# A positional conv split between VectorE, ScalarE and GpSimd, and a Winograd unit started before the last attention jobs are done

## What is computed

```
x = x + depthwise_conv3x3(x, pos_w) + pos_b            # positional conv
blk = mean over 8 x 8 blocks of x (49 per image)
scores = lin(gelu(lin(blk, s1)), s2); idx = top 4 of the 49
y_cmp = mha(x, blk, blk);  y_sel = mha(x, blk[idx], blk[idx])
y_win = attention of each pixel over its 7 x 7 window (edge padded)
g = softmax(lin(layernorm(x), g_w))                     # three gates
y = g0 * y_cmp + g1 * y_sel + g2 * y_win + x
t = depthwise_conv3x3(lin(y, pin_w), dw_w)              # 128 -> 512 channels
x1, x2 = halves of t
out = layernorm(y + lin(gelu(x1) * x2, pout_w))
```

## Time and profile before

| | |
|---|---|
| median of 3 runs | 791.99 us (790.29 to 796.1) |
| the profiled execution | 791.16 us |
| its span | 789.1 us |
| TensorE matmul busy | 691.7 us (88%) |
| VectorE busy | 571.2 us (72%) |
| ScalarE busy | 393.0 us (50%) |
| GpSimd busy | 213.0 us (27%) |

### The profile page before, as it was taken

The page is one execution under the profiler, slowest core; times in us unless marked ns, Lnnn a source line. Parts: engine busy times, 40 slices in busy tenths (PEclk is TensorE's granted clock), DMA queues, the critical chain, the costliest instruction groups (busy, mean ns, idle before and its releaser), DMA issues.

```text
span 789.1 us, 19122 instructions
## 1 busy us (share of the span) xinstructions
PE 691.7 (88%) x7549; PEld 461.3 (58%) x7549; DVE 571.2 (72%) x860; ACT 393.0 (50%) x855; POOL 213.0 (27%) x365
## 2 busy tenths in 40 slices
PE   3979899999888788898888788888799999999994
PEld 2557477777566666675666566666444555455552
DVE  6982788888898675565675565666158989999942
ACT  2077777676764244343444344445333152547565
POOL 2050255555653014411111101111710436200000
PEclk9989999999999897878989896989699999999998
DMA  5000245555489887767777677651100000001001
GB/s 233 0 1 1 67 124 151 148 142 143 139 156 173 185 153 138 136 125 131 141 146 151 129 133 143 136 99 46 37 2 0 0 1 0 1 20 42 20 20 61
DMA packets 81605, 72.50 MB, mean 92 GB/s; under 512 B 11586, under 2 KB 80107, under 8 KB 81006
## 3 DMA queue, kind: packets, MB, share of 16 engines
q1 hardware_dynamic: 61358, 47.03, 24.9%
q10 hardware_dynamic: 20160, 24.26, 16.7%
HBM read 47.39 MB, written 21.57 MB: 87 GB/s over the span
## 4 chain that ended last, share of the span: by engine, by line
PE 45%; DVE 22%; ACT 12%; DMA 8%; issue 8%; ACTq 3%; SPq 2%; DVEq 0%
PE banks L938 13%; PE banks L761 8%; PE banks L871 6%; DVE FP L1212 5%; DMA Q<-nT 5%; PE banks L856 4%; DVE mx L1356 3%; DVE wn L1321 3%; ACTq L355 3%; DVE AC L1212 2%; ACT SEB L1063 2%; PE banks L889 2%; PE banks L834 2%; DMA FP<-nT 2%; ACT banks L1043 1%
## 5 line engine op out<-in xcount | busy, mean ns | idle before, releaser
L1321 DVE TENSOR_REDUCE wn<-banks 112x2 f32<-112x560 f32 x224 | 164.3, 739 | 89.9 <-PE banks L761 87.4
L1088 ACT ACTIVATE P<-banks 98x448 f32<-98x448 f32 x224 | 119.2, 541 | 149.5 <-PE banks L856 118.1
L938 PE MATMUL banks<-FP,PTB 128*128 128x392 f32 x384 | 129.4, 493 | 1.0 <-DVE c L1344 0.9
L1212 DVE SCALAR_TENSOR_TENSOR AC<-XT,vec,AC 128x1540 f32<-128x1540 f32 (+5 forms) x48 | 115.1, 2400 | 1.1
L871 PE MATMUL banks<-P,Vw 84*17 84x56 f32 (+1 forms) x3584 | 97.5, 232 | 8.8 <-ACT OB L1101 6.9
L938 PEld LDWEIGHTS banks<-FP,PTB 128*128 128x128 f32 x384 | 72.8, 190 | 55.5 <-DVE c L1344 1.6
L761 PE MATMUL banks<-K,Q 126*112 126x280 bf16 x288 | 71.6, 335 | 9.0 <-DVE wn L1321 8.6
L856 PE MATMUL banks<-Q,K 128*128 128x56 bf16 x1152 | 60.8, 197 | 17.4 <-DMA Q<-nT 12.7
L856 PEld LDWEIGHTS banks<-Q,K 128*128 128x128 bf16 x1152 | 56.0, 104 | 28.0 <-DMA Q<-nT 15.5
L871 PEld LDWEIGHTS banks<-P,Vw 84*17 84x17 f32 (+1 forms) x3584 | 57.5, 104 | 20.6 <-issue 9.7
L504 POOL TENSOR_TENSOR pk<-pr,pk 128x434 bf16<-128x434 f32 (+1 forms) x42 | 42.8, 1018 | 89.9 <-ACT pk L1033 89.9
(11 more groups left out here) (228 smaller groups left out, 1140.8 us busy)
## 6 DMA issues: line engine op xcount, KB each, us to landing
K<-k_parts ACTq DMA_DIRECT2D x24, 434.0 KB, 5.4
k_parts<-pk SPq DMA_DIRECT2D x28, 325.5 KB, 4.6
Vw<-v_rows SPq DMA_DIRECT2D x112, 52.1 KB
Q<-q_parts ACTq DMA_DIRECT2D x48, 112.0 KB, 6.0
FP<-k_parts ACTq DMA_DIRECT2D x12, 434.0 KB, 5.3
Vw<-v_rows SPq DMA_DIRECT2D x112, 44.6 KB
q_parts<-pk SPq DMA_DIRECT2D x14, 336.0 KB, 2.6
v_rows<-vst SPq DMA_DIRECT2D x14, 263.5 KB
```

The costliest lines, as they stand in the source:

```text
L938: last = mm(bank(2 + place_in_unit, C, ZPIX), WT[:, dy, part, C * grp:C * (grp + 1)], D[:, part, QROWS * q + dy:QROWS * (q + 1) + dy, :].r ...
L1088: a(P[q % 4][0:HKEYS[half], :], PS[0:HKEYS[half], 4 + q % 2, 0:HEADS * SUB], ACT.Exp).then_inc(sem("w_exp"), 1)
L1212: return ve.scalar_tensor_tensor(out=o, in0=src(ro + dy, rn, co + dx, cn), scalar=v(wcol + t), in1=o, op0=ALU.mult, op1=ALU.add)
L1321: ve.tensor_reduce(wn[tl % 2][:, 2 * hp:2 * hp + 2], src, AX.X, ALU.max, negate=True).then_inc(sem("w_slot_read"), 1)
```

## The change

**Positional conv.** TensorE takes four bands of image 1 (`PEB` = 4) and VectorE the last three. Of image 0 VectorE does the first 32 rows (`SPLIT`). The last 24 rows, three bands, are started by ScalarE with the scaled copy, and for each of eight taps ScalarE writes a product into one of two buffers (`products`, in `PTB`), which GpSimd adds onto `FP`. GpSimd's three summing additions go; VectorE sums both images along the rows, after both convs. GpSimd copies image 1 into `XT`, and ScalarE only image 0.

**Feed-forward.** The first conv unit's four parts and the first part of unit 1 are issued inside the loop over the steps, around the last two jobs' D and Y. `outputs(0)` stands in VectorE's loop ahead of job 13's D. The last slots and the first `pin_bands` use other PSUM banks.

```diff
-        PEB = 5
+        PEB = 4
+        SPLIT = 4 * BLOCK
 ...
# GpSimd
+            outer = FP[:, 0, PAD + SPLIT:PAD + SIDE, PAD:PAD + SIDE]
+            for n, t in enumerate(SIDE_TAPS):
+                dy, dx = TAPS[t]
+                rn, co, cn = SIDE - SPLIT - max(0, dy), max(0, -dx), SIDE - abs(dx)
+                pool.wait_ge(sem("diag"), 9 + n + 2)
+                pool.wait_ge(sem("consts"), 5 + n)
+                o = outer[:, 0:rn, co:co + cn]
+                g.tensor_tensor(o, o, products[n % 2][:, 0:rn, co:co + cn], ALU.add).then_inc(sem("consts"), 1)
 ...
-                if m == 0:
-                    by2 = FP[:, 0, mid, mid].rearrange("p r (n e) -> p r n e", e=2)
 ...
+            for b in range(BANDS):
 ...
+                g.tensor_copy(dst, src).then_inc(sem("tile_order1"), 1)
 ...
# TensorE
+                if q == STEPS + 9:
+                    pe.wait_ge(sem("w_exp"), STEPS)
+                    pe.wait_ge(sem("w_slot_read"), pa_order["Y", JOBS - 3] + 1)
+                    pe.wait_ge(sem("wt_ready"), 2)
+                    pe.wait_ge(sem("d_border"), 1)
+                    pe.wait_ge(sem("d_ready"), 2)
+                    conv_part(0, 0)
+                    conv_part(0, 1)
                 if q == STEPS + 11:
+                    conv_part(0, 2)
                     pe.wait_ge(sem("w_y"), JOBS - 1)
-                    pe.wait_ge(sem("w_exp"), STEPS)
-                    pin_bands(0, 0, (4, 5))
+                    pe.wait_ge(sem("w_out"), SUBS * JOBS)
+                    pin_bands(0, 0, (6, 7), range(3))
+                    conv_part(0, 3)
+                    pin_bands(0, 0, (6, 7), range(3, BANDS))
+                if q == STEPS + 25:
+                    conv_part(1, 0)
 ...
-            pe.wait_ge(sem("w_y"), JOBS)
-            pe.wait_ge(sem("wt_ready"), 2)
-            pe.wait_ge(sem("d_border"), 1)
-            pe.wait_ge(sem("t_read"), BANDS)
 ...
# ScalarE
+            act.wait_ge(sem("x0_loaded"), 16)
+            x0 = X[:, 0, :].rearrange("p (r c) -> p r c", c=SIDE)
+            a(FP[:, 0, PAD + SPLIT:PAD + SIDE, PAD:PAD + SIDE], x0[:, SPLIT:, :], ACT.Identity, scale=c1[:, 0:1], bias=v(V_POSB)).then_inc(sem("diag"), 1)
+            for n, t in enumerate(SIDE_TAPS):
+                dy, dx = TAPS[t]
+                rn, co, cn = SIDE - SPLIT - max(0, dy), max(0, -dx), SIDE - abs(dx)
+                if n >= 2:
+                    act.wait_ge(sem("consts"), 5 + n - 1)
+                a(products[n % 2][:, 0:rn, co:co + cn], x0[:, SPLIT + dy:SPLIT + dy + rn, co + dx:co + dx + cn], ACT.Copy, scale=v(V_POSW + t)).then_inc(sem("diag"), 1)
 ...
+                if n in (2, 4):
+                    pos_read(n // 2 - 1)
+            pos_read(2)
 ...
# VectorE
-                first = BLOCK * PEB if m else 0
+                first, end = (BLOCK * PEB, SIDE) if m else (0, SPLIT)
 ...
+                    dve.wait_ge(sem("consts"), 5 + len(SIDE_TAPS))
                     dve.wait_ge(sem("pos_read"), PEB)
 ...
+            for m in range(IMAGES):
+                inner = FP[:, m, PAD:PAD + SIDE, PAD:PAD + SIDE]
+                ve.tensor_reduce(bs1[:, m, :, :], inner.rearrange("p r (b c) -> p r b c", c=BLOCK), AX.X, ALU.add).then_inc(sem("conv_done"), 1)
 ...
+                if q == STEPS + 12:
+                    outputs(0)
```

More of the change, by code:

```diff
@@ L195, in build @@
         TP = SEB[:, 0:9 * HID].rearrange("p (y x o) -> p y x o", y=3, x=3)
+        products = [PTB[:, n * 24 * SIDE:(n + 1) * 24 * SIDE].rearrange("p (r c) -> p r c", c=SIDE) for n in range(2)]
         def xt(img):
@@ L824, in _, with pin_bands @@
             pe.wait_ge(sem("w_zeroed"), 1)
-            def pin_bands(m, grp, banks):
+            def pin_bands(m, grp, banks, bands=range(BANDS)):
                 at0 = BANDS * (IMAGES * m + grp)
@@ L830, in pin_bands @@
                     pe.wait_ge(sem("t_read"), at0)
-                for b in range(BANDS):
+                for b in bands:
                     if b >= 2:
@@ L834, in pin_bands, with conv_part @@
                     mm(bank(banks[b % 2], C, BAND), w("pin", C, C * grp), X[:, m, b * BAND:(b + 1) * BAND], start=True, stop=True).then_inc(sem("t_proj"), 1)
[L836 removed]
+            def conv_part(u, place_in_unit):
+                n, grp = divmod(u, 2)
+                q, part = n % QUARTERS, WINO[place_in_unit]
+                if u >= 1:
+                    pe.wait_ge(sem(("x2_m1", "x2_sums", "x2_even", "x2_odd")[place_in_unit]), u)
+                for dy in range(3):
+                    last = mm(bank(2 + place_in_unit, C, ZPIX), WT[:, dy, part, C * grp:C * (grp + 1)],
+                              D[:, part, QROWS * q + dy:QROWS * (q + 1) + dy, :].rearrange("p r c -> p (r c)"), start=(dy == 0), stop=(dy == 2))
+                last.then_inc(sem("x2_m"), 1)
+            for q in STEP_RANGE:
+                if q == STEPS + 9:
[6 more added lines that the diff above has]
+                    conv_part(0, 1)
                 if q == STEPS + 11:
+                    conv_part(0, 2)
                     pe.wait_ge(sem("w_y"), JOBS - 1)
[L839 to L840 removed]
+                    pe.wait_ge(sem("w_out"), SUBS * JOBS)
[4 more added lines that the diff above has]
+                    conv_part(1, 0)
                 if q == 1:
@@ L924, in z_variance @@
                 last.then_inc(sem("z_var"), 1)
-            for u in range(UNITS):
-                n, grp = divmod(u, 2)
-                m, q = divmod(n, QUARTERS)
+            for u in range(1, UNITS):
+                m, q = divmod(u // 2, QUARTERS)
                 pe.wait_ge(sem("d_ready"), QUARTERS * m + min(q + 2, QUARTERS))
-                for place_in_unit, part in enumerate(WINO):
+                for place_in_unit in range(int(u == 1), len(WINO)):
                     if place_in_unit == 2 and u - 1 in ZAT:
@@ L934, in _ @@
                         z_centre(ZAT[u])
[L935 to L940, removed]
+                    conv_part(u, place_in_unit)
                 if u in PINS:
+                    pe.wait_ge(sem("w_y"), JOBS)
                     pin_bands(*PINS[u], (0, 1))
@@ L966, in _, with tile_order, pos_read @@
                 a(diag[:, t, :], cst[:, CI:CI + C], ACT.Copy, scale=c1[:, 0:1] if t == 4 else v(V_POSW + t)).then_inc(sem("diag"), 1)
[L968 to L971, removed]
+            def tile_order(first, last):
+                for b in range(first, last):
+                    src = FP[:, 0, PAD + BLOCK * b:PAD + BLOCK * (b + 1), PAD:PAD + SIDE].rearrange("p r (s c) -> p s r c", c=SUBC)
+                    dst = XT[:, 0, b * BAND:(b + 1) * BAND].rearrange("p (s r c) -> p s r c", s=SUBS, c=SUBC)
                     a(dst, src, ACT.Copy).then_inc(sem("tile_order"), 1)
-            act.wait_ge(sem("p_gl"), 1)
-            a(cgw[:, C:GW], PS[:, 7, 0:3], ACT.Copy).then_inc(sem("gl_copied"), 1)
-            for b in range(PEB):
+            def pos_read(b):
                 act.wait_ge(sem("pos_conv"), b + 1)
@@ L1485, in _ @@
                     product(ZAT[u])
-                outputs(u)
+                if u:
+                    outputs(u)
             next(todo, None)
```

79 lines of the change are left out of this document (37 added, 42 removed).

## The result

The median went from 791.87 to 805.23 us (four runs, 798.47 to 809.08), a ratio of 1.0154 with an interval of 1.0111 to 1.0196: 1.5% slower, and 4 us above the forecast of 801.0. It lies inside the range that was forecast (794 to 806), by 0.8 us. The profiled execution took 804.07 us, 12.9 more than that of before.

What follows compares the result with a forecast made beforehand. VectorE was taken to bound the positional conv; in the feed-forward part TensorE and VectorE both ran nearly without a gap. 791.16 + 8.0 (positional conv) + 1.8 (feed-forward) = 801.0 us, range 794 to 806.

Steps and rivals of the forecast that it cites:

- What bounds the first stage: Positional conv: VectorE is the bound until `blk_ready` at 56.9 us; TensorE's bands and GpSimd's sums end earlier.
- VectorE's own work, 31.8 us: Positional conv: VectorE's taps and scaled copies alone take 31.8 us after the change, where before it was 43.6.
- The additions cost their time: Positional conv: GpSimd's additions and VectorE's taps take turns, so all eight additions lengthen VectorE's chain, by 16.5 us.
- rival A: Positional conv: GpSimd's additions run beside the taps, so the conv gives -6.2 us and the total is near 785; chance 0.09.
- Their price, 16.5 us: Positional conv: eight additions of 10,442 elements at 1.76 ns each, less 1.8 us, cost VectorE 16.5 us.
- rival C: Positional conv: the new additions are slower than the old sums, +10.5 us and more, 803.5 to 807 in all; chance 0.15.
- The reductions, +3.3: Behind the convs: image 0's sums leave GpSimd and become a second long reduction on VectorE, adding 3.3 us.
- ScalarE's order and the copies into `XT`: First stage: waits between ScalarE and GpSimd hold nobody else, and GpSimd's padding and `XT` copies cost the reduction nothing.
- Edit 2, TensorE's lead: Feed-forward change: TensorE is 1.5 us ahead after three matmuls of unit 1, 3 if its clock comes back earlier.
- Edit 2, VectorE's taps +9.3: Feed-forward change: VectorE's taps begin 9.3 us later, `outputs(2)` ends +3.2, `outputs(5)` starts +1.9; the whole change costs +1.8.
- Rival B: Feed-forward: TensorE sets the pace and VectorE's late taps are absorbed, -1.5 to -3 us, 797 in all; chance 0.18.
- edit 1: The positional conv change as a whole: `blk_ready` and the kernel 8.0 us later, bounds -6.2 and +14.2.

Runs made afterwards that it cites:

- e9: e1 with VectorE's conv of image 0 held until GpSimd's eight additions are done; 821.44 us in one run.
- e3: e1 with each of GpSimd's eight additions replaced by a fill of the product buffer (output not the reference's); 785.18 us, ratio 0.9889 to the kernel before.
- e1: The kernel before with only the positional conv half of the change; 805.19 us, ratio 1.0143 to the kernel before.
- e2: The kernel before with only the feed-forward half of the change; 793.01 us, ratio 0.9996 to the kernel before.
- e4: The kernel before with GpSimd's three summing additions of image 0 moved behind the conv of image 1; 792.16 us, ratio 0.9974 to the kernel before.

## Why the prediction was right, step by step

*What bounds the first stage.* Right. TensorE and ScalarE had room, and VectorE's chain moved `blk` by what it was longer itself. That shift stays whole: the last `banks<-PTB,VP` matmuls before the window attention come 10.6 us later too.

*VectorE's own work, 31.8 us.* Right to 0.1: in e9 the two convs are 39.08 to 70.88.

*The additions cost their time (against rival A).* Right, and shown from both sides. With additions a tap is 2.4 us too long; with GpSimd only writing the product's buffers at the same places (e3) none is. The Trainium skill, SBUF — State Buffer, section "Who interferes with whom", has the port pair shared by VectorE and GpSimd as an exclusive lock. By that rule the additions are paid in full, and e1 and e9 agree, save for the 0.38 us. Beside two-input instructions it excepts GpSimd instructions that only write, and e3's taps agree with that too.

*Their price, 16.5 us.* This is the term that was mis-sized, and rival C, given 0.15, is what happened: 58.9 - 8.1 - 31.8 = 19.0 us, 2.4 each. I took 1.76 ns an element from the sums since they stood in the same stage and layout. Nothing in them said that another pair of operands has the same price, and the nearest row with an own addition and other operands pointed up. By e9, the bound from the earlier trace rows was too high (2.78 us alone, where 2.35 ns would be 3.1). Theirs is most of the difference of 4 us between forecast and result: the first stage is +10.6 instead of +8.0.

*The reductions, +3.3.* Right: from 58.92 to 67.60 is 8.7 us, and before 51.57 to 57.02, 5.4.

*ScalarE's order and the copies into `XT`.* Right, they hid: GpSimd's copies run beside the reductions and end at 63.9, and TensorE's wait is for `blk`.

*Edit 2, TensorE's lead.* Too small: 1.5 forecast, "3 if the clock comes back earlier", and it is 3.4 in e2. There the clock came back 6 us behind D (at 569), where I had counted 7.4, and the six matmuls took 6.7 us, where I had 7.5. In after the clock didn't fall at D at all, so the half clock "with conv matmuls in it" isn't there.

*Edit 2, VectorE's taps +9.3 and what follows.* Right in kind. From D of job 12 to the first tap it is 15.24 us in before, 22.8 in e2 (+7.6) and 20.7 in after. The wait ahead of `outputs(2)` is gone, as forecast, and TensorE is held from there. But `outputs(2)` ends only 1.4 us later in e2 instead of 3.2, and `outputs(5)` starts 0.4 later instead of 1.9, so edit 2 costs 0.0 to +0.5 instead of +1.8, by kernels with the same clock. The medians say +0.9 (ratio of after less that of e1) and -0.3 (e2), each give or take 3 to 5 us, and can't tell this from 1.8. Rival B, that the lateness is absorbed, is nearer here than my sum; but its gain of 1.5 to 3 us isn't there either, since the lead goes in three waits.

*The total.* By the stages it is 791.2 + 10.6 + 0.0 = 801.8, against 801.0 forecast. That they come so close is luck: edit 1 was taken 2.6 us too low and edit 2 some 1.5 too high. The profile has 804.1, since the window attention took 4.4 us more and the clock behind D gave back 1.9; the median has 805.2. The profile's 2.3 us over the stages lie where the forecast had no term, in the window attention, which spans 13.6 us over the twelve profiles; whether edit 1 has a share in it isn't settled, and the median's 3.4 us can't be placed.

## What to carry to other kernels

A two-input fp32 operation on GpSimd beside VectorE's two-input taps doesn't share their work here, it stands in their queue: giving GpSimd an element costs VectorE about 1.8 ns to save 1.05. Price such a hand-over by the other engine's duration with those operands alone, measured once, and not by another instruction's slope. Work moved into a waiting engine's gap pays only if the next reader keeps up: look for the engine that frees the buffers before counting the gap as gain. Compare a stretch only between profiles in which the clock was at the same level.

## What was not expected of the hardware

The 0.38 us: VectorE loses less than the whole addition, by the same amount at four sizes from 0.84 to 2.90 us (e4, e9). It fits that GpSimd's padding copies, which last 0.36 us alone, cost the taps nothing: beside four of them e9's eight taps took 12.88 us, 1.61 each. The copies did wait, a tap each. GpSimd in e9, one copy beside taps and one with none:

```profile
58.05 1.71 POOL L496 COPY FP<-FP 128x168 f32<-128x168 f32 x1
71.07 0.36 POOL L495 COPY FP<-FP 128x168 f32<-128x168 f32 x1 [8.04 <-DVE c L1244]
```

I had not thought of the scaled copy as something that GpSimd could hold, since it reads one tensor only. The one of 1,344 elements took 3.23 us in after beside an addition and 0.98 in e9 without one. The Trainium skill, SBUF — State Buffer, section "Who interferes with whom", counts a `tensor_scalar` in if it runs in a two-port mode; these two numbers agree. A fill held it too, unlike the taps: 1.29 us in e3. VectorE's timeline in e9:

```profile
56.93 0.98 DVE L1238 TENSOR_SCALAR FP<-X,c,vec 128x1344 f32<-128x1344 f32 x1
```

The contiguous addition is slower than the one with 55-element rows, 2.99 against 2.78 us for 1,320 elements.

TensorE's clock at the hand-over differs between profiles. With a pause of 3.55 us ahead of D it was at 1.2 GHz in D (e2), and in after, with 1.26 us, it stayed at 2.4 GHz. The pause ahead of D doesn't settle it alone: e9 has the same 1.26 us, and there it went to 1.2 GHz 2 to 3 us behind D. In this stretch after has conv matmuls, and e9 waits for the normalisation and for X. Two rows of e2 and one of after show it (TensorE by stretches: busy, records, granted clock, DMA share, GB/s):

```profile
568.00:569.00 1.00, 1.00 (x3) 0.50 0.00 0
569.00:570.00 1.00, 1.00 (x4) 1.00 0.00 0
```
```profile
581.00:582.00 1.00, 0.36 (x1) 1.00 0.07 14
```
